# Linear stage of a two-layer graph network: blocks fetched by TensorE and by GpSimd in groups of four turns (4, 4, 4, 5 and 12, 12, 12, 11)

## The chip, the cores and the metric

The kernel runs on one core of a Trainium2 chip. The metric is device time in microseconds (us), median of repeated runs. Lower is better.

## What is computed

Two graph layers over 6250 nodes and 200000 edges that are sorted by their destination. The first is three attention layers; the second, which the change touches, sends a message along every edge and adds the messages up by destination:

```python
h = jnp.maximum(_layernorm(x, axis=-1), 0.0)
# second graph layer
ea = edge_attr @ W_edge.T + b_edge            # 16 -> 64 channels, for each edge
msg = jax.nn.relu(x[src] + ea)                # x is h here; a row of 64 for each edge
agg = jax.ops.segment_sum(msg, dst, num_segments=x.shape[0])
h = (1.0 + GIN_EPS) * x + agg
h = h @ W1.T + b1                             # batch norm, relu, second matmul follow
```

## The kernel before

Each of the 128 partitions owns a run of J = 1568 edges. They are worked in 98 turns of G = 16 edges for each partition, so a turn has 16 blocks of 128 rows `x[src]`. Turns go in pairs (`PAIRS` = 49): turn k = 0 and turn k = 1 of a pair have buffers of their own (`xl[:, k]`, `hot[k]`, `staged[k]`, `idx[:, k]`, `attr[:, k]`). Below, the turns of the linear stage are numbered 0 to 97; even numbers are k = 0.

The rows come in two ways. GpSimd (POOL) gathers blocks from the table in HBM, one indirect DMA for each block (`turn_gathers`, L516). TensorE fetches the other blocks (`pe_gather`, L604): a one-hot matrix times the table kept in SBUF, 14 matmuls for each block. A block's matmuls leave eight candidate rows side by side in a bank of PSUM; VectorE (DVE) halves them three times (`select_rows`, L1158), and ScalarE (ACT) copies the result into `xl` (`rows_copied`). In the attention layers TensorE fetches 4 blocks of an even turn and 5 of an odd one (`FETCHED`); in the linear stage it fetches 4 in every turn (`LINEAR`), and POOL gathers 12.

TensorE's blocks of a turn are split in two shares, q = 0 and q = 1. Each has a step of its own on ACT (`widen`, which turns the 16-bit one-hot matrix in `staged` into the operand `hot`), on TensorE, on DVE and on ACT again. With 4 blocks both shares have 2.

One turn t of the linear stage, by engine:

- ACT (`linear_turn`): `turn_masks`, the two `rows_copied` of t, the factors of the sums (`same_part`, `v_lin`), the relu (L946), `hand_out_linear` (copy and store of turn t-1's sums), then `widen_both` for turn t+2, into `hot[k]`. Then turn t+1 begins with its `turn_masks`.
- DVE (`linear_turn`): `select_rows` of both shares of t (waits for `turn_masks` and for TensorE), `linear_sums` of t-1 (three scans, L1200), then the addition of `xl` and the edge product (L1437), which waits for both `rows_copied`, for POOL's gathers of t (`s_xl`) and for the edge product (`s_ea`). It then frees `xl[:, k]` and `pE`.
- TensorE: for each share waits for `widen` (`s_wide`) and for the copy out of the same bank of the turn before (`s_rows`), then its matmuls; then the four matmuls of the edge product (L678).
- POOL: waits until turn t-2 has used `xl[:, k]` (`s_used`), then gathers.
- SP (the queue of the loads): when the gathers of t have landed (`s_xl`), loads the indices (L387) and the one-hot matrix (L390) of turn t+2; when the edge product of t is done, its edge attributes (L378).

The order on every engine is written out by hand; all waits are on counting semaphores. The loops run over pairs, and the wait values are computed in registers from the loop's counter.

Of the kernel before, what the change touches and what calls it, by code (L numbers as in the profile page):

```python
# [37 lines left out]
N, C, H, O = 6250, 64, 4, 16  # L38
E, KE = 200000, 16
LAYERS = 3  # L40
G = 16
J = 1568
TURNS = J // G
PAIRS = TURNS // 2
FETCHED = (4, 5)
PAIR = sum(FETCHED)
MOST = max(FETCHED)
# [3 lines left out]
LIN_SHARES = tuple(((n - LINEAR, n - 2), (n - 2, n)) for n in FETCHED)  # L51
LIN_SHARE_BANK = (0, 2)
GD = tuple(G - n for n in FETCHED)
LGD = G - LINEAR
EP = P * J
# [27 lines left out]
def build(nc, t):  # L83
    with ExitStack() as ctx:
# [239 lines left out]
        K_TURN, K_ENDS, K_NODE = 5, 10, 4 * GROUPS  # L324

        block = ctx.enter_context(nc.Block())


        @block.sync
        def _(sp):  # L330
# [46 lines left out]
            def load_attr(turn, k):  # L377
                sp.dma_start(attr[:, k, :], t["attr_t"][bass.ds(turn, 1)].rearrange("a p q -> (a p) q")).then_inc(s_attr[k], 16)  # L378
# [114 lines left out]
            for k in range(2):  # L493
                sp.dma_start(attr[:, k, :], t["attr_t"][k]).then_inc(s_attr[k], 16)
            with sp.Fori(0, PAIRS - 1) as i:
                for k in range(2):
                    sp.wait_ge(s_xl[k], (i + 1) * (16 * LGD) + LAYERS * PAIRS * 16 * GD[k])
                    load_idx(2 * i + (2 + k), k)
                    sp.wait_ge(s_wide[1], 2 * i + (LAYERS * TURNS + k + 1))
                    load_hot(2 * i + (2 + k), k)  # L500
                    sp.wait_ge(s_ea[k], i + 1)
                    load_attr(2 * i + (2 + k), k)
            result = t["out"].rearrange("(p b) c -> p b c", p=P)
            for g in range(GROUPS):
# [9 lines left out]
        def _(pool):  # L514
# [42 lines left out]
            pool.wait_ge(s_tab_l, 16 * GROUPS * (LAYERS + 1))  # L557
            with pool.Fori(0, PAIRS) as i:
                for k in range(2):
                    turn_gathers(i + LAYERS * PAIRS, k, range(LGD))  # L560
            pool.wait_ge(s_stored[0], (LAYERS + 1) * (16 * PAIRS))
# [5 lines left out]


        def share(k, q, n=TW):

            shares, banks = (LIN_SHARES, LIN_SHARE_BANK) if n == C else (SHARES, SHARE_BANK)
            lo, hi = shares[k][q]
            return lo, hi, banks[q]

# [9 lines left out]
        def _(pe):  # L584
# [6 lines left out]

            def pe_gather(copied, q, k, n=TW):

                pe.wait_ge(s_rows[q], copied)
                pe.sem_inc(s_passed, 1)
                if q:
                    pe.wait_ge(s_pg[q - 1], copied + 1)
                    pe.sem_inc(s_passed, 1)
                lo, hi, bank = share(k, q, n)
                for a in range(lo, hi):  # L600
                    for m in range(GB):
                        for part in range(PARTS):
                            rows = xl_part[part][:, m * GB * TW:(m + 1) * GB * TW].rearrange("p (b c) -> p b c", b=GB)
                            product = pe.matmul(pG[:, bank + a - lo, 0:GB * n], hot[k][:, m, a * P:(a + 1) * P], rows[:, :, 0:n],  # L604
                                                start=(m == 0 and part == 0), stop=(m == GB - 1 and part == PARTS - 1))
                product.then_inc(s_pg[q], 1)
# [60 lines left out]
            pe.sem_inc(s_passed, 1)  # L667
            with pe.Fori(0, PAIRS) as i:
                for k in range(2):
                    for q in range(2):  # L670
                        pe.wait_ge(s_wide[q], 2 * i + (LAYERS * TURNS + k + 1))
                        pe.sem_inc(s_passed, 1)
                        pe_gather(2 * i + (LAYERS * TURNS + k), q, k, C)
                    pe.wait_ge(s_attr[k], (i + 1) * 16)
                    pe.wait_ge(s_ea_used, 2 * i + k)
                    pe.sem_inc(s_passed, 1)
                    for q in range(2):
                        product = pe.matmul(pE[:, q * 512:(q + 1) * 512], attr[:, k, q * P:(q + 1) * P], w_blk[:, :],  # L678
                                        start=True, stop=True)
                    product.then_inc(s_ea[k], 1)  # L680
            pe.wait_ge(s_fin, LAYERS + 1)
            pe.transpose(pT[0:C, 0, 0:P], fin_s[:, 0:C], ident[:, :]).then_inc(s_finT, 1)
# [34 lines left out]
        def _(act):  # L717
# [14 lines left out]

            def rows_copied(selected, used, q, k, n=TW):

                act.wait_ge(s_sel[q], selected)
                act.wait_ge(s_used[k], used)
                lo, hi, bank = share(k, q, n)
                copy(xl[:, k, GD[k] + lo:GD[k] + hi, 0:n], pG[:, bank:bank + hi - lo, 0:n]).then_inc(s_rows[q], 1)
# [16 lines left out]

            def widen(ready, filled, used, k, q, n=TW):

                act.wait_ge(ready[k], filled)
                act.sem_inc(s_passed, 1)
                act.wait_ge(s_pg[q], used)  # L760
                act.sem_inc(s_passed, 1)
                lo, hi, bank = share(k, q, n)
                copy(hot[k][:, :, lo * P:hi * P], staged[k][:, :, lo * P:hi * P]).then_inc(s_wide[q], 1)

            def widen_both(ready, filled, used, k, n=TW):
                for q in range(2):
                    widen(ready, filled, used, k, q, n)

# [163 lines left out]

            def linear_turn(i, k, first=False, last=False):
                use = i + LAYERS * PAIRS
# [4 lines left out]
                turn_masks(i, k)  # L939
                rows_copied(turn_all + 1, use, 0, k, C)  # L940
                rows_copied(turn_all + 1, use, 1, k, C)
                act.wait_ge(s_sums, turn_all)
# [6 lines left out]
                if not last:  # L949
                    widen_both(s_hot_in, i * 16 + ((LAYERS - 1) * PAIRS + 2) * 16, turn_all + 1, k, C)  # L950

            widen_both(s_hot_in, (LAYERS - 1) * (PAIRS * 16) + 16, LAYERS * TURNS, 0, C)
            act.wait_ge(s_parts, (LAYERS + 1) * GROUPS)
            act.wait_ge(s_tab_l, 16 * GROUPS * (LAYERS + 1))
            widen_both(s_hot_in, (LAYERS - 1) * (PAIRS * 16) + 16, LAYERS * TURNS, 1, C)
            linear_turn(0, 0, first=True)
            linear_turn(0, 1)
            with act.Fori(1, PAIRS - 1) as i:
                for k in range(2):
                    linear_turn(i, k)  # L960
            for k in range(2):
                linear_turn(PAIRS - 1, k, last=True)
            hand_out_linear((LAYERS + 1) * TURNS, (LAYERS + 1) * (16 * PAIRS) - 16, TURNS - 1, 1)
# [31 lines left out]
        def _(dve):  # L995
# [156 lines left out]

            def select_stage(k, q, stage, width=TW):
                lo, hi, bank = share(k, q, width)
                n = (3, 2, 1)[stage] * width
                at = (4, 2, 1)[stage] * width
                rows = pG[:, bank:bank + hi - lo, :]
                return dve.copy_predicated(rows[:, :, 0:n], over(pick_turn[:, k, stage, lo:hi], n), rows[:, :, at:at + n])  # L1158

            def select_rows(gathered, masked, selects, k, q, width=TW):  # L1160


                dve.wait_ge(s_mask, masked)
                dve.sem_inc(s_passed, 1)
                dve.wait_ge(s_pg[q], gathered)
                dve.sem_inc(s_passed, 1)
                select_stage(k, q, 0, width).then_inc(s_pick, 1)
                dve.wait_ge(s_pick, selects * 2 + 1)
                dve.sem_inc(s_passed, 1)
                select_stage(k, q, 1, width).then_inc(s_pick, 1)  # L1170
                dve.wait_ge(s_pick, selects * 2 + 2)
                dve.sem_inc(s_passed, 1)
                select_stage(k, q, 2, width).then_inc(s_sel[q], 1)

# [247 lines left out]

            def linear_turn(i, k, first=False):
                turn = 2 * i + k
                turn_all = 2 * i + (k + LAYERS * TURNS)
                selects = 4 * i + (2 * k + 2 * LAYERS * TURNS)
                select_rows(turn_all + 1, turn_all + 1, selects, k, 0, C)
                select_rows(turn_all + 1, turn_all + 1, selects + 1, k, 1, C)
                if not first:
# [4 lines left out]
                dve.wait_ge(s_rows[1], turn_all + 1)  # L1434
                dve.wait_ge(s_xl[k], (i + 1) * (16 * LGD) + LAYERS * PAIRS * 16 * GD[k])
                dve.wait_ge(s_ea[k], i + 1)
# [4 lines left out]

            linear_turn(0, 0, first=True)
            linear_turn(0, 1)
            done(tt(x[:], x[:], blocks(b2_all[:, :], B), ALU.add)); last()
            with dve.Fori(1, PAIRS) as i:
                for k in range(2):
                    linear_turn(i, k)
            dve.wait_ge(s_lin_relu, TURNS)
# [112 lines left out]
```

## Time and profile before

| | us |
|---|---|
| median of three runs (6514.9 to 6515.72) | 6515.55 |
| profiled execution, its own time | 6514.41 |
| its span in the profile | 6512.6 |
| busy over the span: TensorE matmul | 5708.2 (88%) |
| busy: VectorE | 5034.3 (77%) |
| busy: ScalarE | 4659.4 (72%) |
| busy: GpSimd | 4777.9 (73%) |

The span is divided into three attention layers and the linear stage, which runs from about 4918 to 6404 us. The busy shares are means over all of these; what the change is worth is decided in the linear stage alone. "Idle before" in a row is the time that the engine stood still just ahead of those instructions, and the arrow names what ended it. "issue" is a release that the profile does not show.

### The profile page before, as it was taken

Reading aid. Unit: us, or ns where it says so; the run is one execution under the profiler, and the core shown is the slowest. Engines: PE = TensorE matmul, PEld = TensorE weight load, DVE = VectorE, ACT = ScalarE, POOL = GpSimd, SP = SyncE. Lnnn points to the kernel's source line nnn. Section 1 sums busy time; section 2 is a strip of 40 time slices with the busy share of each in tenths; the row PEclk is TensorE's granted clock in tenths of the full one; section 3 lists DMA queues with packets and bytes.
Section 4 is the critical chain, followed back from the end, with each engine's and each line's share of the span. In section 5 each row is a group of like instructions: output and inputs, shape, how many; then the busy total and the mean of one; then the engine's idle time right before and its main releaser. Section 6 shows DMA issues by size and latency. Waiting matters only on the chain.

```text
span 6512.6 us, 95522 instructions
## 1 busy us (share of the span) xinstructions
PE 5708.2 (88%) x25094; PEld 4712.9 (72%) x25094; DVE 5034.3 (77%) x7554; ACT 4659.4 (72%) x6121; POOL 4777.9 (73%) x4960
## 2 busy tenths in 40 slices
PE   2699999999679999999958999999967999999996
PEld 1577777777558888888847888888856777777774
DVE  8699999999759999999948999999984433444333
ACT  1588888888548888888828888888864555555553
POOL 3777777777677777777767777777767777777774
PEclk9899999999779999999969999999988999999996
DMA  9577777777435555555525555555543444444441
GB/s 391 189 235 235 235 235 233 236 234 233 148 114 177 182 174 177 182 175 176 183 67 169 183 174 177 183 174 177 183 127 110 139 139 142 142 140 142 143 141 52
DMA packets 453279, 1147.43 MB, mean 176 GB/s; under 512 B 159660, under 2 KB 224798, under 8 KB 417668
## 3 DMA queue, kind: packets, MB, share of 16 engines
q1 hardware_dynamic: 279472, 919.26, 39.2%
q0 software_dynamic: 159376, 175.97, 14.5%
q10 hardware_dynamic: 14404, 51.92, 2.0%
q8 instruction: 7, 0.11, 0.0%
q14 instruction: 20, 0.16, 0.0%
HBM read 750.45 MB, written 396.27 MB: 176 GB/s over the span
## 4 chain that ended last, share of the span: by engine, by line
DVE 32%; POOL 23%; issue 22%; ACT 18%; DMA 3%; ACTq 1%; DVEq 1%; PE 1%; POOLq 0%; SPq 0%
POOL sb_xl L516 17%; DVE pG L1158 8%; DVE sb_s_run L1200 7%; ACT sb_turn_out L719 5%; ACT pB L719 4%; ACT sb_v_in L719 4%; ACT sb_hot L719 4%; DVE sb_e_in L1223 3%; DVE sb_lr L1221 3%; DVE sb_s L1219 3%; POOL sb_hot_f L516 3%; DMA sb_xl<-xl_table,sb_idx 2%; POOL marks L520 2%; DVE sb_s L1437 2%; DVE sb_v_g L1254 1%
## 5 line engine op out<-in xcount | busy, mean ns | idle before, releaser
L604 PE MATMUL pG<-sb_xl_parts,sb_hot 128*128 128x476 f32 (+1 forms) x24010 | 5326.0, 380 | 447.6 <-ACT sb_xl L719 334.9
L604 PEld LDWEIGHTS pG<-sb_xl_parts,sb_hot 128*128 128x128 f32 x24010 | 4499.9, 189 | 1316.3 <-issue 720.2
L516 POOL DMA_INDIRECT sb_xl<-xl_table,sb_idx x4557 | 4383.2, 962 | 1412.1 <-issue 1385.3
L1158 DVE COPY_PREDICATED pG<-sb_pick_turn,pG 128x408 f32<-128x408 int32 (+7 forms) x2352 | 1072.0, 457 | 936.2 <-ACT sb_pick_turn L719 808.7
L719 ACT ACTIVATE sb_hot<-sb_wide 128x1792 fp32r<-128x1792 bf16 (+1 forms) x784 | 1426.7, 1833 | 105.4 <-ACT sb_turn_out L719 69.3
L1200 DVE TENSOR_TENSOR_SCAN sb_s_run<-pB,sb_v_in 128x272 f32<-128x272 f32 (+3 forms) x1470 | 1102.9, 778 | 25.0 <-ACT sb_turn_out L719 4.0
L719 ACT ACTIVATE sb_turn_out<-sb_s_run 128x1088 f32<-128x1088 f32 (+3 forms) x395 | 835.6, 2115 | 11.4 <-DVE sb_s_run L1200 11.1
L719 ACT ACTIVATE sb_xl<-pG 128x136 f32<-128x136 f32 (+4 forms) x826 | 247.0, 302 | 677.0 <-DVE pG L1158 568.9
L1197 DVE TENSOR_TENSOR_SCAN pB<-sb_same_c,pB 128x1024 f32<-128x1024 f32 x294 | 672.4, 2287 | 0.1
L719 ACT ACTIVATE pB<-sb_mark 128x960 f32<-128x960 f32 x294 | 562.4, 1913 | 81.6 <-DMA sb_mark<-marks 63.0
L719 ACT ACTIVATE sb_v_in<-sb_v_g 128x1024 f32<-128x1024 f32 x291 | 600.5, 2063 | 0.0
L1219 DVE TENSOR_TENSOR sb_s<-sb_xl,pB 128x1024 f32<-128x1024 f32 x294 | 353.7, 1203 | 44.0 <-DMA sb_xl<-xl_table,sb_idx 42.8
L1223 DVE TENSOR_REDUCE sb_e_in<-sb_lr 128x64 f32<-128x1024 f32 x294 | 359.2, 1222 | 10.0
L1221 DVE SCALAR_TENSOR_TENSOR sb_lr<-sb_s,pB 128x1024 f32<-128x1024 f32 x294 | 358.9, 1221 | 10.1
L1254 DVE TENSOR_TENSOR sb_v_g<-sb_xl,pB 128x1024 f32<-128x1024 f32 x291 | 355.2, 1221 | 10.0
L719 ACT ACTIVATE sb_same_c<-sb_same 128x960 f32 (+1 forms) x294 | 305.2, 1038 | 70.1 <-DVEq L1143 62.0
L719 ACT ACTIVATE sb_v_in<-sb_s_run 128x68 f32<-128x68 f32 (+1 forms) x389 | 126.4, 325 | 238.2 <-DVE sb_s_run L1200 238.2
L946 ACT ACTIVATE sb_v_in<-sb_s 128x1024 f32<-128x1024 f32 x98 | 198.3, 2023 | 30.0 <-DVE sb_s L1437 29.7
L719 ACT ACTIVATE pB<-sb_same 128x374 f32 (+1 forms) x98 | 48.3, 492 | 216.8 <-DVE sb_s_run L1200 216.8
L520 POOL DMA_INDIRECT marks<-sb_XR,sb_first_edge x147 | 146.4, 996 | 61.8 <-issue 61.8
L678 PE MATMUL pB<-sb_w_blk,sb_wide 128*128 128x512 f32 x392 | 184.2, 592 | 0.0
L516 POOL DMA_INDIRECT sb_hot_f<-state_rows,sb_last_edge x147 | 141.3, 961 | 44.8 <-issue 44.8
(237 smaller groups left out, 2278.0 us busy)
## 6 DMA issues: line engine op xcount, KB each, us to landing
state_rows<-sb_turn_out SPq DMA_DIRECT2D x294, 576.0 KB
sb_wide<-hots SPq DMA_DIRECT2D x147, 1120.0 KB
sb_mark<-marks SPq DMA_DIRECT2D x294, 512.0 KB
sb_wide<-hots SPq DMA_DIRECT2D x147, 896.0 KB
sb_xl<-xl_table,sb_idx POOLq DMA_INDIRECT x4557
sb_wide<-codes SPq DMA_DIRECT2D x49, 1120.0 KB
hots<-sb_wide SPq DMA_DIRECT2D x49, 1120.0 KB, 4.3
marks<-sb_hot_f SPq DMA_DIRECT2D x32, 1568.0 KB
```

Source lines behind the costliest of these rows:

```text
L516: return pool.indirect_dma_start(out=dst, out_offset=None, in_=table, in_offset=bass.IndirectOffsetOnAxis(ap=index, axis=0))
L520: return pool.indirect_dma_start(out=table, out_offset=bass.IndirectOffsetOnAxis(ap=index, axis=0), in_=src, in_offset=None)
L604: product = pe.matmul(pG[:, bank + a - lo, 0:GB * n], hot[k][:, m, a * P:(a + 1) * P], rows[:, :, 0:n], start=(m == 0 and part == 0), stop ...
L719: return act.activation(out, in_, ACT.Copy)
L946: act.activation(v_lin[:, :, 1:G1], s[:].rearrange("p g c -> p c g"), ACT.Relu).then_inc(s_lin_relu, 1)
L1158: return dve.copy_predicated(rows[:, :, 0:n], over(pick_turn[:, k, stage, lo:hi], n), rows[:, :, at:at + n])
L1197: dve.tensor_tensor_scan(xr_flat, same_c[:].rearrange(flat3), xr_flat, 0.0, ALU.mult, ALU.add).then_inc(s_xr, 1)
L1200: return dve.tensor_tensor_scan(s_run[:, lo:hi, :].rearrange(flat3), factors[:, 0:(hi - lo) * G1], v_in[:, lo:hi, :].rearrange(flat3), 0.0 ...
L1219: tt(s[:], xl[:, k, :, 0:C], xr.rearrange("p c g -> p g c"), ALU.add).then_inc(s_added, 1)
L1221: done(dve.scalar_tensor_tensor(out=lr[:], in0=s[:], scalar=0.0, in1=blocks(a_turn, G), op0=ALU.max, op1=ALU.mult)); steps_done()
L1223: done(red(e_turn.rearrange("p h g -> p g h"), lr[:].rearrange("p g (h o) -> p g h o", h=H), AX.X, ALU.add)); steps_done()
L1254: tt(v_g[:].rearrange("p g (h o) -> p g h o", h=H), xl_heads, weights, ALU.mult).then_inc(s_used[k], 1)
```

## The change

In the linear stage the turns go in groups of four. TensorE fetches 4 blocks in three of them and 5 in the fourth; POOL gathers 12, 12, 12 and 11. The turns with five are 1, 5, 9, ... 97: 25 of the 98. In such a turn share q = 0 has 3 blocks (`SHARES[1]`), and q = 1 has 2 as before. Turn pair 0 is written out ahead of the loops, and each loop body holds four turns (`QUADS` = 24) where it held two. Share q = 1 uses banks 3 and 4 of `pG` in every turn of the stage (it was 2 and 3), and the counts that SP and DVE wait for (`s_xl`) follow the uneven numbers.

```diff
-LIN_SHARE_BANK = (0, 2)
-LGD = G - LINEAR
+QUADS = PAIRS // 2
+LIN_LANDED = (G - MOST, 2 * G - LINEAR - MOST, 3 * G - LINEAR - 2 * MOST)
...
+        def share(k, q, n=TW, five=False):
+            lo, hi = (LIN_SHARES if n == C and not five else SHARES)[k][q]
+            return lo, hi, SHARE_BANK[q]
+        def five_blocks(k, j):
+            return k == 1 and j % 2 == 0
+        def lin_landed(k, quad, j):
+            attention = LAYERS * PAIRS * 16 * GD[k]
+            if k == 0:
+                return quad * (2 * (G - LINEAR) * 16) + (attention + (j + 1) * (G - LINEAR) * 16)
+            return quad * (LIN_LANDED[1] * 16) + (attention + LIN_LANDED[j] * 16)
...
-            with sp.Fori(0, PAIRS - 1) as i:
+            def linear_loads(quad, j):
+                i = 2 * quad + j
                 for k in range(2):
-                    sp.wait_ge(s_xl[k], (i + 1) * (16 * LGD) + LAYERS * PAIRS * 16 * GD[k])
+                    sp.wait_ge(s_xl[k], lin_landed(k, quad, j))
...
+            linear_loads(0, 0)
+            with sp.Fori(0, QUADS - 1) as quad:
+                for j in (1, 2):
+                    linear_loads(quad, j)
+            linear_loads(QUADS - 1, 1)
...
-            with pool.Fori(0, PAIRS) as i:
+            def linear_gathers(quad, j):
                 for k in range(2):
-                    turn_gathers(i + LAYERS * PAIRS, k, range(LGD))
+                    turn_gathers(2 * quad + (LAYERS * PAIRS + j), k, range(G - LINEAR - five_blocks(k, j)))
...
-            with pe.Fori(0, PAIRS) as i:
+            def linear_products(quad, j):
+                i = 2 * quad + j
...
-                        pe_gather(2 * i + (LAYERS * TURNS + k), q, k, C)
+                        pe_gather(2 * i + (LAYERS * TURNS + k), q, k, C, five_blocks(k, j))
...
-            def linear_turn(i, k, first=False, last=False):
+            def linear_turn(quad, j, k, first=False, last=False):
+                i = 2 * quad + j
...
-                rows_copied(turn_all + 1, use, 0, k, C)
-                rows_copied(turn_all + 1, use, 1, k, C)
+                rows_copied(turn_all + 1, use, 0, k, C, five_blocks(k, j))
+                rows_copied(turn_all + 1, use, 1, k, C, five_blocks(k, j))
...
-                    widen_both(s_hot_in, i * 16 + ((LAYERS - 1) * PAIRS + 2) * 16, turn_all + 1, k, C)
+                    widen_both(s_hot_in, i * 16 + ((LAYERS - 1) * PAIRS + 2) * 16, turn_all + 1, k, C, five_blocks(k, j + 1))
...
-            def linear_turn(i, k, first=False):
+            def linear_turn(quad, j, k, first=False):
+                i = 2 * quad + j
+                five = five_blocks(k, j)
...
-                select_rows(turn_all + 1, turn_all + 1, selects, k, 0, C)
-                select_rows(turn_all + 1, turn_all + 1, selects + 1, k, 1, C)
+                select_rows(turn_all + 1, turn_all + 1, selects, k, 0, C, five)
+                select_rows(turn_all + 1, turn_all + 1, selects + 1, k, 1, C, five)
...
-            with dve.Fori(1, PAIRS) as i:
-                for k in range(2):
-                    linear_turn(i, k)
+            with dve.Fori(0, QUADS) as quad:
+                for j in (1, 2):
+                    for k in range(2):
+                        linear_turn(quad, j, k)
```

## Rows read from the trace of the kernel before

**Rows 1.** Busy time of each engine in a stretch of the linear stage.

```profile
core 0: us, PE busy (x) PEld busy (x) DVE busy (x) ACT busy (x) POOL busy (x), PEclk, DMA share, GB/s
5300.00:5500.00 200.00, 182.18 (x800) 147.82 (x799) 78.90 (x130) 115.73 (x119) 151.24 (x161) 1.00 0.47 141
```

**Rows 2.** Who waited for whom, longest in total first, 5300 to 5700 us.

```profile
DVE pG L1158 <- ACT sb_pick_turn L719: 227.3, 27, 8.5
```

**Rows 3.** Groups by line and shape, 5300 to 5700 us.

```profile
L516 POOL DMA_INDIRECT sb_xl<-xl_table,sb_idx x321 | 302.9, 944 | 97.8 <-issue 96.0 <-DVEq L1439 1.8
L719 ACT ACTIVATE sb_hot<-sb_wide 128x1792 fp32r<-128x1792 bf16 x54 | 88.8, 1691 | 21.3 <-ACT sb_turn_out L719 21.3
L1158 DVE COPY_PREDICATED pG<-sb_pick_turn,pG 128x384 f32<-128x384 int32 x53 | 29.8, 562 | 227.3 <-ACT sb_pick_turn L719 227.3
L1158 DVE COPY_PREDICATED pG<-sb_pick_turn,pG 128x128 f32<-128x128 int32 x52 | 15.4, 296 | 7.6
```

**Rows 4.** Timeline: turn 5 and turn 95, SP's load and DVE's addition.

```profile
5011.43 0.33 SPq L387 DMA_DIRECT2D sb_idx<-src_edges  x1
5012.16 1.19 DVE L1437 TENSOR_TENSOR sb_s<-sb_xl,pB 128x1024 f32<-128x1024 f32 x1
...
6359.80 0.33 SPq L387 DMA_DIRECT2D sb_idx<-src_edges  x1
...
6368.44 1.20 DVE L1437 TENSOR_TENSOR sb_s<-sb_xl,pB 128x1024 f32<-128x1024 f32 x1
```

**Rows 5.** Timeline of turns 38 and 39, around the ring of ACT and DVE.

```profile
5506.09 5.98 PE L604 MATMUL pG<-sb_xl_parts,sb_hot 128*128 128x448 f32 x28 [1.21 <-ACT sb_xl L719]
...
5509.44 1.19 DVE L1437 TENSOR_TENSOR sb_s<-sb_xl,pB 128x1024 f32<-128x1024 f32 x1
...
5512.22 6.00 PE L604 MATMUL pG<-sb_xl_parts,sb_hot 128*128 128x448 f32 x28
5512.59 2.02 ACT L719 ACTIVATE sb_turn_out<-sb_s_run 128x1024 f32<-128x1024 f32 x1
5515.47 3.29 ACT L719 ACTIVATE sb_hot<-sb_wide 128x1792 fp32r<-128x1792 bf16 x2 [0.87 <-ACT sb_turn_out L719]
5518.05 1.88 PE L678 MATMUL pB<-sb_w_blk,sb_wide 128*128 128x512 f32 x4
5518.67 0.20 ACT L719 ACTIVATE sb_pick_turn<-sb_pick 128x15 int32 x1
5519.13 3.12 DVE L1158 COPY_PREDICATED pG<-sb_pick_turn,pG 128x384 f32<-128x384 int32 x6 [8.50 <-ACT sb_pick_turn L719]
5522.15 2.51 DVE L1200 TENSOR_TENSOR_SCAN sb_s_run<-pB,sb_v_in 128x374 f32<-128x374 f32 x3
5524.58 1.20 DVE L1437 TENSOR_TENSOR sb_s<-sb_xl,pB 128x1024 f32<-128x1024 f32 x1
5525.81 2.02 ACT L946 ACTIVATE sb_v_in<-sb_s 128x1024 f32<-128x1024 f32 x1 [0.29 <-DVE sb_s L1437]
```

**Rows 6.** Groups by line and shape in the third attention layer, 4000 to 4400 us.

```profile
L719 ACT ACTIVATE sb_hot<-sb_wide 128x1792 fp32r<-128x1792 bf16 x42 | 71.1, 1693 | 0.0
L719 ACT ACTIVATE sb_hot<-sb_wide 128x2688 fp32r<-128x2688 bf16 x14 | 34.2, 2445 | 0.0
L1158 DVE COPY_PREDICATED pG<-sb_pick_turn,pG 128x612 f32<-128x612 int32 x14 | 11.2, 800 | 0.4
```

**Rows 7.** Timeline of turn 97, the last.

```profile
6386.16 6.01 PE L604 MATMUL pG<-sb_xl_parts,sb_hot 128*128 128x448 f32 x28
...
6392.31 1.58 DVE L1158 COPY_PREDICATED pG<-sb_pick_turn,pG 128x384 f32<-128x384 int32 x3 [1.18 <-PE pG L604]
```

**Rows 8.** Timeline of turns 1 and 2, at the start of the stage.

```profile
4946.48 1.58 DVE L1158 COPY_PREDICATED pG<-sb_pick_turn,pG 128x384 f32<-128x384 int32 x3 [1.23 <-PE pG L604]
4950.40 1.20 DVE L1437 TENSOR_TENSOR sb_s<-sb_xl,pB 128x1024 f32<-128x1024 f32 x1
4966.35 1.22 DVE L1437 TENSOR_TENSOR sb_s<-sb_xl,pB 128x1024 f32<-128x1024 f32 x1 [0.92 <-DMA sb_xl<-xl_table,sb_idx]
```

More of the change, by code:

```diff
@@ L557, in _ @@
             pool.wait_ge(s_tab_l, 16 * GROUPS * (LAYERS + 1))
-            with pool.Fori(0, PAIRS) as i:
+            def linear_gathers(quad, j):
                 for k in range(2):
-                    turn_gathers(i + LAYERS * PAIRS, k, range(LGD))
+                    turn_gathers(2 * quad + (LAYERS * PAIRS + j), k, range(G - LINEAR - five_blocks(k, j)))
+            linear_gathers(0, 0)
+            with pool.Fori(0, QUADS) as quad:
+                for j in (1, 2):
+                    linear_gathers(quad, j)
             pool.wait_ge(s_stored[0], (LAYERS + 1) * (16 * PAIRS))
@@ L566, in _ @@
                     gather(node_rows[:, b, 0:C], agg_rows, last_edge[:, b:b + 1]).then_inc(s_nrow[g], 16)
[L569 to L573, printed above, removed]
         def place(psum, i):
@@ L590, in _, with pe_gather @@
             pe.wait_ge(s_contT, 3)
-            def pe_gather(copied, q, k, n=TW):
+            def pe_gather(copied, q, k, n=TW, five=False):
                 pe.wait_ge(s_rows[q], copied)
@@ L598, in pe_gather @@
                     pe.sem_inc(s_passed, 1)
-                lo, hi, bank = share(k, q, n)
+                lo, hi, bank = share(k, q, n, five)
                 for a in range(lo, hi):
@@ L672, in _ @@
                         pe.sem_inc(s_passed, 1)
-                        pe_gather(2 * i + (LAYERS * TURNS + k), q, k, C)
+                        pe_gather(2 * i + (LAYERS * TURNS + k), q, k, C, five_blocks(k, j))
                     pe.wait_ge(s_attr[k], (i + 1) * 16)
-                    pe.wait_ge(s_ea_used, 2 * i + k)
+                    if not isinstance(i, int) or i or k:
+                        pe.wait_ge(s_ea_used, 2 * i + k)
                     pe.sem_inc(s_passed, 1)
@@ L680, in _ @@
                     product.then_inc(s_ea[k], 1)
+            linear_products(0, 0)
+            with pe.Fori(0, QUADS) as quad:
+                for j in (1, 2):
+                    linear_products(quad, j)
             pe.wait_ge(s_fin, LAYERS + 1)
@@ L731, in _, with rows_copied @@
             act.activation(stat[:, 2, :], stat[:, 1, :], ACT.Sqrt).then_inc(s_std, 1)
-            def rows_copied(selected, used, q, k, n=TW):
+            def rows_copied(selected, used, q, k, n=TW, five=False):
                 act.wait_ge(s_sel[q], selected)
                 act.wait_ge(s_used[k], used)
-                lo, hi, bank = share(k, q, n)
+                lo, hi, bank = share(k, q, n, five)
                 copy(xl[:, k, GD[k] + lo:GD[k] + hi, 0:n], pG[:, bank:bank + hi - lo, 0:n]).then_inc(s_rows[q], 1)
@@ L754, in turn_marks, with widen @@
                 copy(xr[:, :, 1:G], mark[:, k, 1:G, :].rearrange("p g c -> p c g")).then_inc(s_xrin, 1)
-            def widen(ready, filled, used, k, q, n=TW):
+            def widen(ready, filled, used, k, q, n=TW, five=False):
                 act.wait_ge(ready[k], filled)
@@ L761, in widen, with widen_both @@
                 act.sem_inc(s_passed, 1)
-                lo, hi, bank = share(k, q, n)
+                lo, hi, bank = share(k, q, n, five)
                 copy(hot[k][:, :, lo * P:hi * P], staged[k][:, :, lo * P:hi * P]).then_inc(s_wide[q], 1)
-            def widen_both(ready, filled, used, k, n=TW):
+            def widen_both(ready, filled, used, k, n=TW, five=False):
                 for q in range(2):
-                    widen(ready, filled, used, k, q, n)
+                    widen(ready, filled, used, k, q, n, five)
             def widen_first(l, i, k, fresh):
@@ L954, in _ @@
             act.wait_ge(s_tab_l, 16 * GROUPS * (LAYERS + 1))
[L955 to L958, printed above, removed]
-                for k in range(2):
-                    linear_turn(i, k)
+            widen_both(s_hot_in, (LAYERS - 1) * (PAIRS * 16) + 16, LAYERS * TURNS, 1, C, five_blocks(1, 0))
+            linear_turn(0, 0, 0, first=True)
+            linear_turn(0, 0, 1)
+            with act.Fori(0, QUADS - 1) as quad:
+                for j in (1, 2):
+                    for k in range(2):
+                        linear_turn(quad, j, k)
             for k in range(2):
-                linear_turn(PAIRS - 1, k, last=True)
+                linear_turn(QUADS - 1, 1, k)
+            for k in range(2):
+                linear_turn(QUADS - 1, 2, k, last=True)
             hand_out_linear((LAYERS + 1) * TURNS, (LAYERS + 1) * (16 * PAIRS) - 16, TURNS - 1, 1)
@@ L1151, in build_one_hot, with select_stage @@
                 ts(staged[k].rearrange("p m e -> p (m e)"), staged_code[k], code_no[:, 0:1], None, ALU.is_equal).then_inc(s_hot[k], 1)
-            def select_stage(k, q, stage, width=TW):
-                lo, hi, bank = share(k, q, width)
+            def select_stage(k, q, stage, width=TW, five=False):
+                lo, hi, bank = share(k, q, width, five)
                 n = (3, 2, 1)[stage] * width
@@ L1158, in select_stage, with select_rows @@
                 return dve.copy_predicated(rows[:, :, 0:n], over(pick_turn[:, k, stage, lo:hi], n), rows[:, :, at:at + n])
-            def select_rows(gathered, masked, selects, k, q, width=TW):
+            def select_rows(gathered, masked, selects, k, q, width=TW, five=False):
                 dve.wait_ge(s_mask, masked)
@@ L1166, in select_rows @@
                 dve.sem_inc(s_passed, 1)
-                select_stage(k, q, 0, width).then_inc(s_pick, 1)
+                select_stage(k, q, 0, width, five).then_inc(s_pick, 1)
                 dve.wait_ge(s_pick, selects * 2 + 1)
                 dve.sem_inc(s_passed, 1)
-                select_stage(k, q, 1, width).then_inc(s_pick, 1)
+                select_stage(k, q, 1, width, five).then_inc(s_pick, 1)
                 dve.wait_ge(s_pick, selects * 2 + 2)
                 dve.sem_inc(s_passed, 1)
-                select_stage(k, q, 2, width).then_inc(s_sel[q], 1)
+                select_stage(k, q, 2, width, five).then_inc(s_sel[q], 1)
             def cut_parts(g, base):
@@ L1434, in linear_turn @@
                 dve.wait_ge(s_rows[1], turn_all + 1)
-                dve.wait_ge(s_xl[k], (i + 1) * (16 * LGD) + LAYERS * PAIRS * 16 * GD[k])
+                dve.wait_ge(s_xl[k], lin_landed(k, quad, j))
                 dve.wait_ge(s_ea[k], i + 1)
@@ L1440, in linear_turn @@
                 dve.sem_inc(s_ea_used, 1)
-            linear_turn(0, 0, first=True)
-            linear_turn(0, 1)
+            linear_turn(0, 0, 0, first=True)
+            linear_turn(0, 0, 1)
             done(tt(x[:], x[:], blocks(b2_all[:, :], B), ALU.add)); last()
-            with dve.Fori(1, PAIRS) as i:
-                for k in range(2):
-                    linear_turn(i, k)
+            with dve.Fori(0, QUADS) as quad:
+                for j in (1, 2):
+                    for k in range(2):
+                        linear_turn(quad, j, k)
             dve.wait_ge(s_lin_relu, TURNS)
```

## The prediction

> **What bounds the kernel now.** The change touches the linear stage alone, so I read the busy time of that stage by stretches, not the shares of the whole span. In a stretch of 200 us TensorE is busy 182 us, POOL 151, ACT 116 and DVE 79, at a granted clock of 1.00, its upper level of 2.4 GHz [rows 1]. No engine is full, and two look suspicious: TensorE at 91%, and POOL, whose gathers stand one behind the other with about 0.30 us of "issue" between them (96.0 of their 97.8 us of idle time) [rows 3].
>
> Next, POOL against the turn. 321 gathers take 302.9 us busy and 97.8 us idle [rows 3], so 1.248 us each and 14.98 us for the 12 of a turn. The turn itself: from the addition of turn 5 to that of turn 95 it is 6368.44 - 5012.16 = 1356.28 us for 90 turns, 15.07 us each [rows 4]. So POOL is faster than the turn by 0.09 us. The reader can see that drift: SP loads new indices as soon as a turn's gathers have landed, and it does so 0.73 us ahead of the addition that uses them in turn 5, but 8.64 us ahead in turn 95 [rows 4]. (8.64 - 0.73) / 90 turns is 0.088 us, the same number from another side. From turn 5 on nothing waits for a gather.
>
> What does set the turn is a ring that goes through ACT and DVE once for each turn. The view of waits names it: DVE's first selection waits for ACT's masks 27 times in 400 us, 227.3 / 27 = 8.4 us each [rows 2], and TensorE ended its second share before those masks came [rows 5]. Along the timeline [rows 5]: masks 5518.67, selections 5519.13 (0.46 later), scans 5522.15 (3.02), addition 5524.58 (2.43), relu 5525.81 (1.23), the relu itself 1.9, then from the copy of the sums to the widening 5515.47 - 5512.59 = 2.88, and from the widening to the next masks 5518.67 - 5515.47 = 3.20. The sum is 15.1, the turn. Each member waits for the one before.
>
> TensorE has slack beside the ring, and only a little: it starts a turn at 5506.09, ends the second share at 5512.22 + 6.00 = 5518.22, ends the edge product at 5519.93, and stands idle 1.21 us ahead of the next turn [rows 5].
>
> **The change, part by part.** I count from the start of TensorE's first matmul of a turn, which follows the ring.
>
> POOL loses 25 gathers, 25 x 1.248 = 31.2 us of its own time [rows 3]. It is ahead of the ring already, so I cost this at nothing. POOL gets further ahead until it waits for the buffer of two turns before. Behind that wait are only its own next gathers, which are needed a turn later. SP's loads are then held by the edge product instead of by the gathers (it issues the attributes in the same order), still most of a turn ahead of the widening. Cover gone, a gather would cost 1.248.
>
> Widening, once in a group, in the turn two ahead of the five: share 0 goes from 1792 to 2688 columns. The attention layers have both forms: 2445 - 1693 = 752 ns [rows 6]. It stands on ACT in the ring with nothing beside it: +0.75.
>
> Selection, in the turn with five: 3 blocks for 2 in share 0. The three steps are 384, 256 and 128 wide and grow to 576, 384 and 192. The slope is (562 - 296) / 256 = 1.04 ns for each column [rows 3], times 192 + 128 + 64 = 384 columns: 0.40 us. The row of 612 columns in the attention layer, 800 ns, agrees with the slope (562 + 228 x 1.04 = 799) [rows 6]. On the ring: +0.40. The copy into `xl` grows too, but DVE goes on to share 1 beside it.
>
> TensorE, in the turn with five: 14 matmuls more, 14 x 6.00 / 28 = 3.0 us [rows 5]. The second share then ends at 12.13 + 3.00 = 15.13 after the start, and a selection that waits for TensorE starts 0.14 to 0.15 after that (6392.31 against 6386.16 + 6.01 = 6392.17 [rows 7]): 15.27. The ring brings DVE to that selection at 5519.13 - 5506.09 = 13.04, plus half of the six selections, 1.54, plus 0.40: 14.98. So TensorE is late by 0.3 us, and that is what is exposed of its 3.0. Afterwards its edge product ends at 13.84 + 3.0 = 16.84, which starts the next turn 1.3 us late; that turn's second share is wanted only 15.0 us after this one's, and there TensorE's slack (14.58 against 12.13 + 0.15) holds 2.3. It has caught up one turn later. The group as a whole agrees: TensorE needs 4 x 13.84 + 3.0 = 58.4 us, the ring 60.3 + 1.15.
>
> So a group pays 0.75 + 0.40 + 0.30 = 1.45 us. There are 23 such turns between the ends (5 to 93): 33.4 us.
>
> The last turn, 97, has no widening ahead of its masks, and DVE waits for TensorE there: 1.18 us idle, ended by PE [rows 7]. All of the 3.0 us is exposed, and 0.75 of the widening in turn 95: +3.75.
>
> The first, turn 1, waits for TensorE as well [rows 8], so its addition comes 3.0 late, at 4953.4. But turn 2's addition had waited 0.92 us for a gather [rows 8], and POOL now lands 1.25 us earlier. Without that wait the ring leads from addition 1 to addition 2 in 4966.35 - 0.92 - 4950.40 = 15.03, so turn 2 is at 4968.4, 2.1 late. From there to turn 5 it took 5012.16 - 4966.35 = 45.81 [rows 4, 8] where 3 turns of 15.07 are 45.2: 0.6 comes back, since POOL's earlier landing also lets SP load the one-hot matrices earlier. Net +1.5.
>
> Loops: bodies of four turns for two. Wait values and addresses come from register instructions, and some stand in the ring. The trace doesn't show the new ones. Bound from rows: consecutive turns take 15.14 and 15.0 by turns (5524.58 - 5509.44 is the first kind [rows 5]; two turns are 30.14, so the other kind is 15.0), so one form costs 0.15 us more than the other. If all turns were of the cheap form the stage would gain 0.075 x 98 = 7 us; if all got 0.15 dearer, it would lose 15. I take 0, as the number of computed values for a turn stays about the same, and keep both ends. The banks, the fewer DMA bytes and the dropped wait of turn 0 cost nothing: none is on the ring.
>
> Sum: 33.4 + 3.75 + 1.5 = 38.6 us. The profiled execution's own time is 6514.41 (its span is 6512.6), 1.1 below the median of 6515.55. 6515.55 + 38.6 = 6554.
>
> **The rivals.**
>
> POOL is the bound (faster). For it: its row of gathers has no gap but the 0.30 us [rows 3], and it is busy 151 of 200 us [rows 1]. Then 25 gathers less would give 31.2 us back: 6484. It decides from the point where a turn's gathers land after its addition is otherwise ready. Against it: the lead of 8.64 us in turn 95 and the 0.09 us by which POOL is faster [rows 4]; a POOL that took no time would leave the ring as long as it is. The Trainium skill, "Perfetto Trace Analysis", section "What 'DMA-bound' means", says that a kernel can be bound by the issuing engine's sequencer, to be known by a track that is solid with DMA slices. POOL's track looks just so here; by that rule the change would be a gain, and the drift in this trace speaks against it. 3%.
>
> TensorE is the bound (slower still). For it: 91% busy, the busiest engine [rows 1]. Each of the 25 turns would pay 3.0: 75 us, 6590. It decides if its slack of 1.21 us in a turn doesn't add up over the group, for instance if the edge product holds it at each turn. Against it: the 1.21 us recur in each turn [rows 5]. 5%.
>
> The loop of four turns. More register work in the ring, 0.15 to 0.3 us in each turn, with the sum above: 6569 to 6583, 8%. Less than now, beyond the 7 us above: under 6545, 6%.
>
> Nothing changes. The additions on ACT and DVE lie in slack that I take for ring, and TensorE's 0.3 too: only the ends pay, 1.5 + 3.0: 6520. Against it: the pieces of the ring sum to the turn [rows 5]. 4%.
>
> **How the numbers follow.** The forecast has 74%, with its own range from 6545 to 6568. The range of 8 in 10 reaches into both sides of the loop rival: 6540 to 6570. What can be told from no change is about 0.2%, 13 us: faster is 3%, same 4%, slower the rest, 93%.
>
> **What would show it.** Right: the addition-to-addition time is 15.0 to 15.15 us in most turns, about 15.8 ahead of a five (the widening of 2688 columns) and about 15.8 in it; in turns with five the second share's selection waits for PE about 0.3 us; the new select forms 576 wide take about 0.76 us; POOL begins to wait for DVE. Wrong: all turns differ by the same amount (the loops); TensorE waited for in turns after a five (the slack doesn't hold); or the lead of the gathers over the addition gone. The weakest numbers are the loops' registers and the 0.3 us, a difference of two sums of 15.

## The result and the profile after

The changed kernel takes 6552.53 us (median of 4 runs, 6550.39 to 6554.8), the kernel before 6515.23 beside it: a ratio of 1.0058 with an interval from 1.0042 to 1.0074, which is 27 to 48 us. The prediction was 6554. Eight of the twelve runs told below (those of about 8700 us or more) were made where the kernel before itself took about 8790 us, because the engines' queues stood still now and then; their whole times aren't compared with 6515, and only the turns in which nothing stood still (the undisturbed ones) are read from them.

Who waited for whom, 5300 to 5700 us of the changed kernel (total, times, longest):

```profile
DVE pG L1194 <- ACT sb_pick_turn L751: 223.6, 26, 9.1
...
POOL sb_xl L540 <- DVEq L1477: 23.6, 14, 2.4
...
ACT sb_hot L751 <- PE pG L628: 5.5, 7, 0.8
DVE pG L1194 <- PE pG L628: 1.5, 7, 0.2
```

Against [rows 2] the first row is the same: DVE's selection waits for ACT's masks in every turn, so the ring still sets the turn, but for the 0.2 us told next. The others are the change. POOL now waits for DVE to free a buffer (L1477), since it needs less time and is ahead. And DVE waits for TensorE in the turns with five, 1.5 / 7 = 0.2 us each. The row in between is no new wait: ACT stands idle 0.78 us there, as long as ahead of any widening (0.87 in [rows 5]), and TensorE's first share merely ended in that time.

The groups by line and shape of the same stretch:

```profile
L540 POOL DMA_INDIRECT sb_xl<-xl_table,sb_idx x304 | 286.8, 944 | 113.1 <-issue 89.5 <-DVEq L1477 23.6
...
L751 ACT ACTIVATE sb_hot<-sb_wide 128x2688 fp32r<-128x2688 bf16 x6 | 14.7, 2451 | 4.2 <-ACT sb_turn_out L751 4.2
...
L1194 DVE COPY_PREDICATED pG<-sb_pick_turn,pG 128x576 f32<-128x576 int32 x7 | 5.3, 763 | 59.0 <-ACT sb_pick_turn L751 59.0
```

The two new forms have the lengths that the forecast used: 2451 ns for 2445, and 763 for a slope that gives 562 + 192 x 1.04 = 762. POOL's gathers take 944 ns, as in [rows 3].

Turns 24 and 25 on the timeline, and the second share of 25, where TensorE is late:

```profile
5302.96 15.04 PE L628 MATMUL pG<-sb_xl_parts,sb_hot 128*128 128x448 f32 x70 [1.94 <-ACT sb_xl L751]
...
5306.31 1.20 DVE L1475 TENSOR_TENSOR sb_s<-sb_xl,pB 128x1024 f32<-128x1024 f32 x1
5307.74 0.33 SPq L403 DMA_DIRECT2D sb_idx<-src_edges  x1
...
5315.93 1.98 DVE L1194 COPY_PREDICATED pG<-sb_pick_turn,pG 128x576 f32<-128x576 int32 x3 [8.42 <-ACT sb_pick_turn L751]
...
5318.15 1.58 DVE L1194 COPY_PREDICATED pG<-sb_pick_turn,pG 128x384 f32<-128x384 int32 x3 [0.24 <-PE pG L628]
...
5322.07 1.20 DVE L1475 TENSOR_TENSOR sb_s<-sb_xl,pB 128x1024 f32<-128x1024 f32 x1
```

Addition to addition is 5322.07 - 5306.31 = 15.76. The second selection starts 5318.15 - 5302.96 = 15.19 after TensorE's start, where the forecast had 15.27.

By the place of the turn in its group, the medians over turns 6 to 93 of addition to addition, from the timeline:

| turn | before | after | forecast |
|---|---|---|---|
| 4n (the five is widened ahead of it) | 14.99 | 15.74 | +0.75 |
| 4n+1 (five blocks) | 15.14 | 15.75 | +0.70 |
| 4n+2 | 14.99 | 15.00 | 0 |
| 4n+3 | 15.14 | 15.14 | 0 |

From addition 0 to addition 97 the stage took 6396.23 - 4934.84 = 1461.39 us before and 6432.33 - 4932.18 = 1500.15 after: +38.8, where the forecast had 38.6. The span grew by 36.0 only, as this execution came to the linear stage 2.7 us earlier (4932.18 against 4934.84), in code that the change doesn't touch.

In two turns, 17 and 57, TensorE was slower. The stretches around turn 17, with the granted clock as the number ahead of the last two:

```profile
5160.00:5177.00 17.00, 14.90 (x63) 11.31 (x61) 6.85 (x12) 9.44 (x10) 12.67 (x14) 1.00 0.51 153
5177.00:5183.00 6.00, 4.82 (x16) 4.35 (x17) 5.29 (x9) 1.52 (x5) 3.38 (x4) 0.72 0.26 50
5183.00:5200.00 17.00, 16.85 (x78) 14.27 (x78) 6.50 (x10) 8.46 (x9) 11.32 (x12) 1.00 0.45 131
```

and its first share and the selection of its second:

```profile
5178.18 10.40 PE L628 MATMUL pG<-sb_xl_parts,sb_hot 128*128 128x448 f32 x42 [1.94 <-ACT sb_xl L751]
...
5194.89 1.58 DVE L1194 COPY_PREDICATED pG<-sb_pick_turn,pG 128x384 f32<-128x384 int32 x3 [1.75 <-PE pG L628]
```

The clock fell to its lower level (1.2 GHz; 0.72 is the mean of the 6 us) for a part of the share, which took 10.40 us where 42 matmuls else take about 9. DVE waited 1.75 us for TensorE in place of 0.24, and the turn took 17.28: 1.5 more. Turn 57 took 17.26. The two make 3.1 of the 38.8 us. The kernel before had no such fall between its additions 0 and 97.

### The profile page after: what moved, and what is told of

Its sections match the earlier page's. It is cut to its first block, busy times and chain, and to the rows that moved or that the text cites. A ratio compares the mean times of both kernels' runs of the same rounds, so it can differ in the third digit from the quotient of the medians.

```text
span 6548.6 us, 95921 instructions
## 1 busy us (share of the span) xinstructions
PE 5772.9 (88%) x25444; PEld 4778.3 (73%) x25444; DVE 5045.8 (77%) x7554; ACT 4680.2 (71%) x6121; POOL 4751.4 (73%) x4935
## 4 chain that ended last, share of the span: by engine, by line
DVE 28%; POOL 24%; issue 21%; ACT 16%; PE 6%; DMA 2%; ACTq 1%; DVEq 1%; POOLq 0%; SPq 0%
POOL sb_xl L540 19%; DVE pG L1194 7%; PE pG L628 6%; DVE sb_s_run L1236 6%; ACT pB L751 4%; ACT sb_turn_out L751 4%; ACT sb_v_in L751 4%; ACT sb_hot L751 4%; POOL sb_hot_f L540 3%; DVE sb_e_in L1259 3%; DVE sb_lr L1257 3%; DVE sb_s L1255 3%; POOL marks L544 2%; DMA sb_xl<-xl_table,sb_idx 2%; DVE sb_s L1475 1%
## 5 line engine op out<-in xcount | busy, mean ns | idle before, releaser
L628 PE MATMUL pG<-sb_xl_parts,sb_hot 128*128 128x476 f32 (+1 forms) x24360 | 5402.9, 380 | 420.2 <-ACT sb_xl L751 307.3
L628 PEld LDWEIGHTS pG<-sb_xl_parts,sb_hot 128*128 128x128 f32 x24360 | 4565.3, 189 | 1287.6 <-issue 685.3
L751 ACT ACTIVATE sb_hot<-sb_wide 128x1792 fp32r<-128x1792 bf16 (+1 forms) x784 | 1445.2, 1857 | 101.5 <-ACT sb_turn_out L751 55.0
L751 ACT ACTIVATE sb_xl<-pG 128x136 f32<-128x136 f32 (+5 forms) x826 | 248.6, 303 | 698.4 <-DVE pG L1194 591.6
```

The source lines that it names most:

```text
L751: return act.activation(out, in_, ACT.Copy)
```

## The experiments

All kernels but one (the earlier masks put on the kernel before) start from the changed one, with loops of four turns. "Quads without fives" below means this edit, which leaves 4 blocks to TensorE and 12 to POOL in every turn:

```diff
         def five_blocks(k, j):
-            return k == 1 and j % 2 == 0
+            return False
...
-            if k == 0:
+            if True:
                 return quad * (2 * (G - LINEAR) * 16) + ...
```

**The loops alone** are that edit and no other.

> Only the loops of four turns and the new banks: 4 blocks by TensorE and 12 by POOL in every turn. Ring theory (the ring through ACT and DVE sets the turn; the new loops cost nothing in it): 98 turns of 15.07 us as before, within 5 us of 6515. Loop theory (the register work of the longer bodies is part of the 37 us): 10 to 37 us above.

8789.54 us beside 8794.32 of the kernel before, ratio 0.9985 (0.9969 to 1.0001). In the turns in which no queue stood still the steps are 15.02, 15.08, 15.00 and 15.15 us (means of 8, 7, 7 and 7 turns, places 4n to 4n+3): the old turn. The longer bodies cost nothing.

**The gathers alone.** Quads without fives in TensorE, DVE and ACT, and POOL leaves a gather out in turns 1, 5, ... 97, so that one block of these turns holds old rows. The counts of `lin_landed` stay the uneven ones of the changed kernel here (the second half of the edit above is not made):

```diff
-  turn_gathers(2 * quad + (LAYERS * PAIRS + j), k, range(G - LINEAR - five_blocks(k, j)))
+  turn_gathers(2 * quad + (LAYERS * PAIRS + j), k, range(G - LINEAR - (k == 1 and j % 2 == 0)))
```

> The loops of four turns, and POOL leaves out one gather in turns 1, 5, ... 97 (11 for 12), with nothing in its place: that block of 25 turns holds old rows. Ring theory: nothing, within 5 us of the run with 12 gathers in each turn; the lead of the gathers over the addition grows faster. POOL theory: 25 x 1.248 = 31 us faster.

8759.9 beside 8794.32, ratio 0.9958 (0.9944 to 0.9972): 34 us less, about what the POOL theory says. But the undisturbed turns take 15.03, 15.09, 15.01 and 15.18 us (places 4n to 4n+3), those of the kernel with the loops alone to 0.03. What is gained lies mainly in the turns in which a queue stood still the longest: 32.5 us in the mean where the loops alone have 33.4, 32 such turns in each. That doesn't tell what bounds an undisturbed turn, so the kernel was run again.

> Loops of four turns, 25 gathers left out with nothing in their place, masks in their old place. Ring theory: within 5 us of the kernel before. POOL theory: 31 us faster.

6511.17 beside 6514.67, ratio 0.9994 (0.9984 to 1.0003). The waits, 5300 to 5700 us:

```profile
DVE pG L1194 <- ACT sb_pick_turn L751: 226.6, 27, 8.5
POOL sb_xl L540 <- issue: 95.8, 310, 0.7
...
POOL sb_xl L540 <- DVEq L1477: 8.1, 5, 1.6
```

31 us of POOL's work are gone and 3.5 came back, at the edge of what can be told from nothing. The ring's row is what it was. The steps of the turns are 14.99, 15.06, 14.99 and 15.14. On the timeline the stage from addition 0 to 97 is 4.2 us shorter (1457.18 for 1461.39): 1.4 at the start, where the step into turn 2 was 14.95 for the 15.95 of before; 2.4 in turns 6 to 93, 1.9 of it in place 4n+1, where the loops alone have a short step too (15.08); and 0.4 in the last turns. POOL as the bound is refuted, but for the first turns.

**The widening alone.** Quads without fives, and ACT widens 3 blocks:

```diff
-  widen_both(s_hot_in, ..., turn_all + 1, k, C, five_blocks(k, j + 1))
+  widen_both(s_hot_in, ..., turn_all + 1, k, C, k == 1 and (j + 1) % 2 == 0)
...
-  widen_both(s_hot_in, ..., 1, C, five_blocks(1, 0))
+  widen_both(s_hot_in, ..., 1, C, True)
```

> The loops of four turns, and ACT widens 3 blocks for 2 in share 0 for the turns 1, 5, ... 97; TensorE, DVE and POOL do 4 and 12 blocks in every turn. Ring theory: 24 x 0.75 = 18 us slower, all in the step from turn 4n+3 to 4n+4; if the two dips of TensorE's granted clock in the changed kernel come from the longer pause that this makes ahead of turns with five, dips may appear here too, and cost nothing or under 1 us each, as TensorE has 2.3 us of slack in a turn of 4. Slack theory: under 5 us.

8794.64 beside 8794.32, ratio 1.0013 (0.9987 to 1.0039). The whole time decides nothing, as 18 us are inside that interval; its undisturbed turns do. The additions of turns 19 and 20, the second in place 4n:

```profile
6902.33 1.22 DVE L1475 TENSOR_TENSOR sb_s<-sb_xl,pB 128x1024 f32<-128x1024 f32 x1 [0.90 <-remote]
...
6918.11 1.20 DVE L1475 TENSOR_TENSOR sb_s<-sb_xl,pB 128x1024 f32<-128x1024 f32 x1
```

15.78 us. The eight undisturbed turns of this place took 15.74 to 15.79, against 15.02 with the loops alone; the other places 15.09, 14.98 and 15.16. So +0.76, in the place that was named.

**The selection alone.** Quads without fives, and DVE selects 3 blocks (its shares no longer fit the masks, so these turns take wrong rows):

```diff
-                five = five_blocks(k, j)
+                five = k == 1 and j % 2 == 0
```

> The loops of four turns, and DVE selects (and so reads, one bank more) 3 blocks for 2 in share 0 of turns 1, 5, ... 97; the rest does 4 and 12. The blocks and their masks are shifted by one, so 25 turns take wrong rows. Ring theory: 25 x 0.40 = 10 us slower, all in the step into turn 4n+1. Slack theory: nothing.

8786.3 beside 8791.51, ratio 0.9996 (0.9987 to 1.0006). The additions of turns 40 and 41:

```profile
7370.48 1.22 DVE L1475 TENSOR_TENSOR sb_s<-sb_xl,pB 128x1024 f32<-128x1024 f32 x1
7385.93 1.20 DVE L1475 TENSOR_TENSOR sb_s<-sb_xl,pB 128x1024 f32<-128x1024 f32 x1
```

15.45 us; the seven undisturbed turns of place 4n+1 took 15.43 to 15.46, against 15.08 with the loops alone: +0.37 for the 0.40 of the forecast. The expected 10 us can't be seen in the whole time of these executions.

**The matmuls alone.** Quads without fives, and TensorE does one block more:

```diff
-                lo, hi, bank = share(k, q, n, five)
-                for a in range(lo, hi):
+                lo, hi, bank = share(k, q, n)
+                for place_no, a in enumerate([*range(lo, hi)] + [lo] * (five and q == 0)):
...
-                            product = pe.matmul(pG[:, bank + a - lo, 0:GB * n], ...
+                            product = pe.matmul(pG[:, bank + place_no, 0:GB * n], ...
...
-                        pe_gather(2 * i + (LAYERS * TURNS + k), q, k, C, five_blocks(k, j))
+                        pe_gather(2 * i + (LAYERS * TURNS + k), q, k, C, k == 1 and j % 2 == 0)
```

> The loops of four turns, and TensorE does 14 matmuls more in share 0 of turns 1, 5, ... 97, into a bank that nobody reads (the first block once more). Ring theory: the second share is late for DVE by 15.13 + 0.14 - 14.58 = 0.7 us in 23 turns between the ends, and by 3.0 in turns 1 and 97 less up to 1.5 that comes back after turn 1: 16 + 5 = 19 to 22 us. TensorE theory: 3.0 in each of 25 turns, 75 us. Nothing: under 6 us (the ends alone).

8800.76 beside 8794.32. Only three turns of place 4n+1 ahead of the last were undisturbed (25, 73 and 85). They took 15.05 to 15.07 us, no more than with the loops alone. But each of them follows a turn of 19.5 us. In turn 24 DVE had stood still while TensorE went on, so TensorE was ahead: it ended the second share of turn 25 at 7012.98 + 6.01 = 7018.99, before the masks at 7019.60. So it was inconclusive, and was run again.

> Loops of four turns, and 14 matmuls more in share 0 of turns 1, 5, ... 97, read by nobody. Ring theory: 0.6 to 0.7 us in each of 23 turns and 3.0 at each end less what comes back: 17 to 22 us slower. TensorE theory: 75. As the pause ahead of the share is the old one here, no dip of the granted clock.

6532.41 beside 6514.67, ratio 1.0027 (1.0016 to 1.0037), 17.7 us slower. Turns 24 and 25:

```profile
5302.61 1.20 DVE L1475 TENSOR_TENSOR sb_s<-sb_xl,pB 128x1024 f32<-128x1024 f32 x1
...
5312.24 1.58 DVE L1194 COPY_PREDICATED pG<-sb_pick_turn,pG 128x384 f32<-128x384 int32 x3 [8.44 <-ACT sb_pick_turn L751]
...
5314.43 1.58 DVE L1194 COPY_PREDICATED pG<-sb_pick_turn,pG 128x384 f32<-128x384 int32 x3 [0.61 <-PE pG L628]
...
5318.35 1.20 DVE L1475 TENSOR_TENSOR sb_s<-sb_xl,pB 128x1024 f32<-128x1024 f32 x1
```

15.74 us, the very step of the changed kernel, with a wait for TensorE of 0.61 us. The steps of the places are 14.99, 15.75, 15.00 and 15.14: TensorE has caught up one turn later. TensorE as the bound (75 us) is refuted, and so is "all of it in slack".

This run also closes the sum. From addition 0 to 97 it took 1479.27 us, 17.9 more than before. With 24 widenings of 0.745 us (17.9, from the steps of place 4n in the changed kernel) and the two falls of the clock (3.1) that is 38.9, where the changed kernel has 38.8. Nothing is left for the longer selection: it lies beside TensorE's lateness.

**The ring made shorter.** If the masks of turn t+1 are cut while turn t is still summed, DVE need not wait for ACT's widening. The edit in ACT's `linear_turn`, on the changed kernel and, likewise, on the kernel before:

```diff
-                act.wait_ge(s_sel[0], turn_all)
-                act.wait_ge(s_sel[1], turn_all)
-                turn_masks(i, k)
+                if first:
+                    act.wait_ge(s_sel[0], turn_all)
+                    act.wait_ge(s_sel[1], turn_all)
+                    turn_masks(i, k)
                 rows_copied(turn_all + 1, use, 0, k, C, five_blocks(k, j))
                 rows_copied(turn_all + 1, use, 1, k, C, five_blocks(k, j))
+                if not (last and k):
+                    turn_masks(i + k, 1 - k)
```

> The kernel before, with ACT's masks for turn t+1 ahead of the sums, relu, copy and widening of turn t instead of behind them. DVE can then select turn t+1 while ACT works. Ring theory: the ring of a turn drops below POOL's 14.98 us, and POOL becomes the bound: 98 x (15.07 - 14.98) = 9 us faster, 6506, with DVE's addition waiting for gathers. If another link holds the turn (TensorE: 13.84 us and a wait), the turn stays at 15.07 or more and nothing is won.

> The changed kernel, with the same earlier masks. Ring theory: the additions of the change on ACT and DVE leave the path, and what POOL gives up counts: a group of four takes 47 x 1.248 = 58.7 us by POOL and 58.4 by TensorE, 14.7 a turn: 98 x (15.07 - 14.7) = 36 us faster than before, 6479, less up to 10 us where POOL and TensorE wait for each other. If the change is bad in itself, it stays slower than the kernel before with early masks.

> The changed kernel with ACT's masks for the next turn ahead of the sums, once more, since the stretches in which TensorE's queue stood still hid most of it in the run before. Where nothing stands still: a group of four takes 58.7 us by POOL and 58.4 by TensorE, so 14.7 a turn and about 36 us less than the kernel before. If turn for turn the additions stay in the path, it is at or above the kernel before.

8761.25 (before: 8791.51), 8773.84 (8791.51) and 8729.08 (8803.3, one run each). All were disturbed, and none of the three expectations can be judged by them. The last two kernels were run once more each, on different chips, each beside the kernel before.

> The kernel before with the earlier masks. POOL theory of this state: the ring is out of the way, 12 gathers of 1.248 us are the bound in every turn, 14.98 us a turn: 98 x 0.09 = 9 us faster than before, 6506, and DVE's addition waits for gathers. The changed kernel with the same masks took 6479; the 27 us between them would be 25 gathers of 1.248 less some waits for TensorE.

The kernel before with earlier masks: 6507.47 beside 6514.67, ratio 0.9988 (0.9979 to 0.9998). Its waits, 5300 to 5700 us:

```profile
DVE pG L1161 <- PE pG L604: 99.5, 33, 4.6
POOL sb_xl L516 <- issue: 95.7, 314, 0.3
DVE sb_s L1440 <- DMA sb_xl<-xl_table,sb_idx: 94.7, 26, 4.1
```

The wait for the masks is gone, and DVE's addition waits for a gather in each of the 26 turns, 3.6 us: POOL is the bound, with a median step of 14.98 us, the 12 gathers of 1.248. DVE's waits for TensorE in the first row come earlier in the turn, at its selections; without them it would wait that much longer for the gather.

> The changed kernel with ACT's masks for the next turn ahead of the sums, in an execution in which TensorE's queue is hoped not to stand still. By the sum: 47 gathers of 1.248 us and 4 x 13.84 + 3.0 us of TensorE in a group, 14.7 us a turn, 6479. POOL and TensorE take turns in holding DVE. If the additions stay in the path: 6515 or more.

The changed kernel with earlier masks: 6479.1 beside 6514.94, ratio 0.9944 (0.9921 to 0.9966), 36 us faster. Its waits:

```profile
DVE pG L1197 <- PE pG L628: 188.1, 55, 5.6
...
DVE sb_s L1478 <- DMA sb_xl<-xl_table,sb_idx: 26.7, 16, 3.1
```

Now TensorE and POOL each hold DVE in some of the turns. From addition 0 to 97 it takes 6359.44 - 4935.74 = 1423.7 us, 14.68 a turn. The version beats both kernels, and the two ratios make the change worth 0.9944 / 0.9988 = 0.9956 there (about 0.993 to 0.998 by their intervals), some 29 us less, where it cost 37 in the old order.

## Why the prediction was right

The bound. The ring was named, and POOL and TensorE were excluded. Taking 25 gathers away gave 3.5 us of 31 (loops of four turns included), taking TensorE 75 us more work cost 17.7, and cutting the ring itself moved the bound to POOL. The lead of the gathers over the addition, from which this was read [rows 4], went on growing after the change, until POOL stopped at its buffers: SP loads the indices of turn 93 14.26 us ahead of the addition in the changed kernel's timeline.

The parts of the sum, in turns 6 to 93: the forecast gave 22 groups 1.45 us each, 31.9. Measured were 32.6, of which 3.1 are the two falls of the clock, which the forecast didn't have; the rest is 29.6, 1.34 for a group. The widening was right (0.75). For the turn with five the sum has 0.40 for the selection and 0.30 for TensorE, which reads as two costs; the runs show that they don't add but that the later one decides. The matmuls alone give the same step as the whole change (15.75), and the selection alone 0.37, under TensorE's lateness. The total of 0.70 came out right since the 0.30 was worked out as what is left behind the 0.40 (15.27 against 14.98); measured it is 0.61 against before and 0.69 against the kernel with the gathers alone, whose turn 4n+1 takes 15.06 for 15.14. The loops, the term set to 0, are the likely reason of that -0.08, as the loops alone show 15.08 there. They moved the last turns too: the steps into 95 and 96 are 14.85 and 14.86 with the gathers alone and 14.86 and 14.87 with the matmuls alone, for 15.14 and 14.99 before. In these kernels ACT's turns 94 and 95 are written out behind the loop; whether that is the reason isn't shown. Together it is about 2.3 us less where nothing else holds these turns, well inside the bound of 7.

The start: +2.9 from addition 0 to 5, where the forecast has 1.5 and one group, 2.95. Turn 1 is 2.88 late; 1.0 us comes back in turn 2 and 0.26 in turn 4. The net was right, but its reason not as it stands: the prediction has turn 2's wait go because POOL lands one gather earlier. The kernel with the matmuls alone, with all its gathers, has the same steps (14.94 into turn 2 and 15.00 into turn 4). With turn 1 as late as that, turn 2's gathers are in time anyway; the kernel with the gathers alone shows that the lighter POOL would have been enough as well.

The end: from addition 93 to 97 6432.33 - 6371.17 = 61.16 for the 6396.23 - 6338.31 = 57.92 of before, +3.2 where the forecast has 3.75; the shorter step into turn 95 is 0.3 of the missing 0.5. The last turn alone shows TensorE's 14 matmuls nearly bare, 15.67 for 12.80; the rows of its second share, beside [rows 7]:

```profile
6422.25 6.01 PE L628 MATMUL pG<-sb_xl_parts,sb_hot 128*128 128x448 f32 x28
...
6428.41 1.58 DVE L1194 COPY_PREDICATED pG<-sb_pick_turn,pG 128x384 f32<-128x384 int32 x3 [3.60 <-PE pG L628]
```

What missed is small and of both signs: 2.3 us too much in the groups, 0.5 at the end, 3.1 too little for the clock. That these cancel is luck: the forecast of the median, 6554 against 6552.5, is better than its parts deserve.

The rule of the Trainium skill, "Perfetto Trace Analysis", section "What 'DMA-bound' means", was the rival with POOL. POOL's track was as solid before as in the kernel with earlier masks, 151.24 and 150.99 us of 200 in the stretch from 5300 to 5500 us; it was the bound only in the second. So a track like this went with that bound here, but it doesn't prove it.

## What to carry to other kernels

Two engines can look full beside a ring that neither is part of; a quick test from one trace is whether an engine's lead over its consumer grows from turn to turn (POOL here), or the engine stands idle anew in each turn (TensorE). Work taken from an engine that pulls ahead like that was worth next to nothing here, and work put on the ring to pay for it cost its full length (0.75 us for 752 ns of widening). Work put on the engine with slack cost only what went beyond the slack (0.6 of 3.0 us). Here cutting the ring first turned the sign: the same exchange of 25 blocks was 37 us of loss before and about 29 us of gain after.

## What the runs showed of the hardware

The granted clock of TensorE fell in the middle of a stage in which it is busy more than nine tenths of the time. One stretch of 10 us around such a fall, first in the kernel before with earlier masks, then in the changed kernel with earlier masks:

```profile
5170.00:5180.00 10.00, 8.08 (x30) 6.52 (x28) 4.17 (x6) 5.54 (x9) 7.56 (x9) 0.83 0.28 50
```

```profile
5576.00:5586.00 10.00, 8.15 (x32) 6.95 (x31) 4.04 (x6) 5.89 (x9) 7.56 (x9) 0.83 0.37 89
```

There were five falls in the first of them (pauses of the weight loads of up to 3.2 us), one in the second (up to 2.6), two in the changed kernel (up to 2.8), and none in the kernels with the gathers and the matmuls alone (up to 2.3 in both). The kernel before had none either, with a regular pause of 2.0 us, but once, in turn 3, one of 3.3. So long pauses go with the falls without being enough for one; no run changed the pause alone in an undisturbed execution, and the cause is not shown. A fall cost 1.5 us in each of the two turns of the changed kernel, both with five blocks, where TensorE had no slack (the wait of 1.75 us above).

In the disturbed executions single engines stood still by about 4 or 18 us, with all that they waited for seemingly done: of the 97 steps of the kernel with the loops alone 33 took up to 15.2 us, 32 took 18 to 20 and 32 took 32 to 36. From turn 39 of the kernel with the loops alone, on the timeline:

```profile
7331.17 0.70 SPq L406 DMA_DIRECT2D sb_wide<-hots  x1
...
7344.67 0.50 PEld L628 LDWEIGHTS pG<-sb_xl_parts,sb_hot 128*128 128x128 f32 x2 [18.66 <-issue]
7344.70 0.56 DVE L1194 COPY_PREDICATED pG<-sb_pick_turn,pG 128x384 f32<-128x384 int32 x1 [19.75 <-remote]
```

TensorE and DVE both wait there for the end of the first share, which TensorE had finished at 7320.40 + 6.00 = 7326.4, and go on together 18 us later. What held the signal stays open.
